# Self-attention stages reordered, head projection in one loop, semaphores cleared in groups

## The chip, the cores and the metric

The program runs on 1 core of a Trainium2 chip. The metric is its time on the device in microseconds (us). It is written in Bass: each engine (TensorE or PE, VectorE or DVE, ScalarE or ACT, GpSimd or POOL, SyncE or SP for DMAs) has an instruction queue of its own, and semaphores alone order one engine against another.

## The reference

Twelve residual layers on x of 32 x 64 tokens x 256 features, each on a layer norm of x. Two of them matter here:

```python
# L1_attn (retention): q, k, v of 16 heads x 16; the (q k) weights are multiplied by a decay matrix,
#   applied to v, normed per batch row and head (mean, variance), scaled, projected with wo
# L2_attn: x + softmax(q k / scale) v Wo + bo, with
def _rmsnorm(x, w):
    rms = jnp.mean(xf * xf, axis=-1, keepdims=True)
    return xf / jnp.sqrt(rms + 1e-06) * w
# q = _rmsnorm(heads of x Wq + bq, wq), k the same; v = x Wv + bv; attention inside each row of 64 tokens
```

## The kernel before

x stays in SBUF as 16 tiles of 128 tokens (2 batch rows of 64) x 256 features. The program is a chain of 34 stages (`stage`, line 31). A stage allocates its tiles and semaphores and opens a `Block` with one instruction list for each engine. The block ends with a barrier of all engines; after it `stage` has GpSimd clear the stage's semaphores (L53) and all engines meet in a second barrier (L54). Weights that outlive a stage are in `held` objects, loaded in the layer norm ahead of their use (`loads=`); that stage can also run their preparation on GpSimd (`prepare=`). Inside a stage the order of each engine is written out by hand, as the order of calls of small helpers (`take(i)`, `flip(i, n)`), i being the tile.

`normed_heads` (L2540) makes queries, keys and values of the second attention. It has two passes over the 16 tiles: first projection in plain fp32 (L2570), bias and squares; then one root and one reciprocal over all tiles (L2591, L2624), and a second loop that scales (DVE, L2628), transposes on PE (L2578, called flip) and stores (ACT, L2596). GpSimd first sets the value tile l2a_v to zero in one instruction (L2558), for which the first values have to wait.

`softmax_attention` (L2632) has per tile: 32 score matmuls on 32 of the 128 rows of the array (`scores`, L2701), maximum and subtraction on DVE (`take`, L2786 and L2790), exponentials on ACT (L2758), their sums and reciprocal on DVE (`add_up`, L2796), scaling on GpSimd (L2675), 8 transposes on all 128 rows (`flip`, L2712), copies of their halves by ACT and DVE (`turned`, L2763 and L2804), 64 matmuls on 64 rows (`attend`, L2726), copies by ACT (`attended`, L2768), 4 matmuls on all 128 rows (`output`, L2736), and the update of x (L2808). The bias of x is added on GpSimd in 4 instructions (L2683) ahead of the first scaling.

`retention_attention` (L2832) has `attend`, `scores`, a matmul for the means (L2905) and one for the variances (L2909), which share one PSUM tile, and `output`. So the matmul of the means of tile i waits until DVE has taken the variances of tile i-1 (`variance`, L3004).

Of the kernel before, what the change touches and what calls it, by code (L numbers as in the profile page):

```python
# [13 lines left out]
P = 128  # L14
BATCH = 32
SEQ = 64
DIM = 256
# [10 lines left out]

@contextmanager
def stage(nc):  # L30
# [22 lines left out]
    nc.clear_and_free_semaphores(sems)  # L53
    nc.all_engine_barrier()  # L54
# [335 lines left out]
class HeadWeights:  # L390

    def __init__(self, sb, sem, d):
        self.d = d
        self.W, self.B, self.WQK = sb("nh_w", [P, KC, 3 * DIM]), sb("nh_bias_rows", [P, 3 * DIM]), sb("nh_rms_weights", [P, 2])
        self.s_w = sem("weights_loaded")

    def load(self, sp):
        d = self.d
        sp.dma_start(self.W[:, :, :], rows_to_sbuf(d["L2_attn_WqkvT"])).then_inc(self.s_w, 16)
# [2140 lines left out]
def normed_heads(nc, XNT, QKT, VA, ident, held):  # L2540

    with stage(nc) as (sb, ps, sem):
        W, B, WQK, s_w = held.W, held.B, held.WQK, held.s_w
        RAW = sb("nh_qk", [P, TILES, 2 * DIM])
        sq = [sb("nh_squares", [P, 2 * DIM]) for _ in range(2)]
        R = sb("nh_rms", [P, TILES, 32])
        psQ = [ps("nh_psq", [P, 512]) for _ in range(2)]
        psV = [ps("nh_psv", [P, 512]) for _ in range(2)]
        psF = [ps("nh_psf", [P, 4, P]) for _ in range(2)]
        s_one, s_p, s_b, s_v, s_sq, s_r = (sem("ones_set"), sem("projected"), sem("qk_ready"),  # L2550
                                                sem("values_ready"), sem("squares_ready"), sem("squares_summed"))
        s_d, s_rt, s_rt2, s_n, s_f, s_out = (sem("dve_step"), sem("mean_squares_ready"), sem("roots_ready"), sem("normed"),
                                             sem("flipped"), sem("stored"))
        with nc.Block() as block:
            @block.gpsimd
            def _(pool):

                nc.gpsimd.memset(VA[:, :, :, :, :], 0.0).then_inc(s_one, 1)  # L2558
                pool.wait_ge(s_one, 1)

            @block.tensor
            def _(pe):

                pe.wait_ge(s_w, 48)
                for t in range(TILES):
                    if t >= 2:
                        pe.wait_ge(s_v, t - 1)
                    for dst, lo, hi in ((psQ[t % 2][:, :], 0, 2 * DIM), (psV[t % 2][:, 0:DIM], 2 * DIM, 3 * DIM)):
                        for c in range(KC):
                            last = nc.tensor.matmul(dst, XNT[:, c, t * P:(t + 1) * P], W[:, c, lo:hi], start=(c == 0),  # L2570
                                                    stop=(c == KC - 1))
                    last.then_inc(s_p, 1)
                for t in range(TILES):
# [3 lines left out]
                    for m in range(4):  # L2577
                        last = nc.tensor.transpose(psF[t % 2][:, m, :], RAW[:, t, m * P:(m + 1) * P], ident[:, :])  # L2578
                    last.then_inc(s_f, 1)

            @block.scalar
            def _(act):
                act.wait_ge(s_w, 48)
# [1147 lines left out]
```

## Time and profile before

| | us |
|---|---|
| time before, median of 3 runs (lowest, highest) | 2920.92 (2920.48, 2927.56) |
| the profiled execution: its time | 2934.49 |
| its span, first to last instruction | 2932.7 |
| PE, DVE, ACT, POOL busy | 2515.0, 1735.1, 1383.3, 637.7 |
| mean granted TensorE clock | 0.922 of 2.4 GHz |

A stage starts when the one before has ended, so the span is a sum of stages, and each stage has its own limit. The granted clock is 1.0 (2.4 GHz) or 0.5 (1.2 GHz); a mean between them is a mixture of both. The stages of the change lie at 1578.7 to 1677.3 (retention), 2194.9 to 2205.5 (layer norm ahead of the heads), 2205.6 to 2276.6 (heads) and 2277.1 to 2389.9 (softmax).

### The profile page before, as it was taken

Reading aid. Unit: us, or ns where it says so; the run is one execution under the profiler, and the core shown is the slowest. Engines: PE = TensorE matmul, PEld = TensorE weight load, DVE = VectorE, ACT = ScalarE, POOL = GpSimd, SP = SyncE. Lnnn points to the kernel's source line nnn. Section 1 sums busy time; section 2 is a strip of 40 time slices with the busy share of each in tenths; the row PEclk is TensorE's granted clock in tenths of the full one; section 3 lists DMA queues with packets and bytes.
Section 4 is the critical chain, followed back from the end, with each engine's and each line's share of the span. In section 5 each row is a group of like instructions: output and inputs, shape, how many; then the busy total and the mean of one; then the engine's idle time right before and its main releaser. Section 6 shows DMA issues by size and latency. Waiting matters only on the chain. (4 is left out here: it accounts for less than half of the span.)

```text
span 2932.7 us, 83514 instructions
## 1 busy us (share of the span) xinstructions
PE 2515.0 (86%) x35763; PEld 2110.2 (72%) x35763; DVE 1735.1 (59%) x3396; ACT 1383.3 (47%) x3431; POOL 637.7 (22%) x826
## 2 busy tenths in 40 slices
PE   6999788999958999999987739977998666999888
PEld 4888455777747999899976539965765554999567
DVE  5777675566655433333335645557885676777663
ACT  3888324455532444444431314426873343777441
POOL 3111002211103200000002122322330534655300
PEclk8999899999989999999998559987998688999999
DMA  2110003212031000000000032332321001111100
GB/s 74 38 35 20 16 7 87 60 32 60 3 90 56 16 17 16 16 16 17 2 24 1 25 126 92 117 105 81 92 78 36 2 2 40 51 51 52 44 1 29
DMA packets 118221, 126.65 MB, mean 43 GB/s; under 512 B 10877, under 2 KB 110153, under 8 KB 117865
## 3 DMA queue, kind: packets, MB, share of 16 engines
q1 hardware_dynamic: 114024, 110.93, 12.3%
q0 software_dynamic: 3840, 10.49, 1.2%
q8 instruction: 282, 4.62, 0.6%
q14 instruction: 75, 0.61, 0.1%
HBM read 105.67 MB, written 15.73 MB: 41 GB/s over the span
## 5 line engine op out<-in xcount | busy, mean ns | idle before, releaser
L1012 ACT ACTIVATE s_ca_probs<-s_ca_scores,s_ca_neg_max 128x256 f32<-128x256 f32 x768 | 353.4, 478 | 36.7 <-DVE s_ca_neg_max L1056 26.1
L1056 DVE TENSOR_REDUCE s_ca_neg_max<-s_ca_scores 128x4 f32<-128x1024 f32 x192 | 234.3, 1222 | 54.6 <-PE s_ca_scores L918 26.8
L935 PE MATMUL s_ca_probs_flipped<-identity,s_ca_probs 128*128 128x128 f32 x1536 | 213.6, 283 | 11.5 <-ACT s_ca_probs L1012 10.5
L2045 DVE COPY s_mx_w_mixed<-s_mx_ps 128x512 f32<-128x512 f32 x256 | 163.6, 684 | 95.4 <-PE s_mx_ps L1892 80.5
L935 PEld LDWEIGHTS s_ca_probs_flipped<-identity,s_ca_probs 128*128 128x128 f32 x1536 | 167.7, 143 | 50.3 <-ACT s_ca_probs L1012 23.2
L2000 ACT COPY s_mx_w_mixed<-s_mx_ps 128x512 f32<-128x512 f32 x256 | 137.2, 589 | 118.6 <-PE s_mx_ps L1879 97.9
L1012 ACT ACTIVATION_READ_ACCUMULATOR s_ca_probs<-s_ca_scores,s_ca_neg_max 128x1 f32 x768 | 160.1, 208 | 0.0
L604 PE MATMUL s_ln_flip<-identity,s_ln_xn 128*128 128x128 f32 x352 | 63.3, 362 | 110.1 <-DVE s_ln_xn L586 109.8
L1019 ACT COPY s_ca_probsT<-s_ca_probs_flipped 128x512 f32<-128x512 f32 x192 | 115.3, 600 | 79.5 <-PE s_ca_probs_flipped L935 79.5
L75 PE MATMUL s_cc_shared<-s_cc_ctxT_low,h_cc_wkv_high 128*128 128x256 f32 x512 | 146.0, 285 | 2.2 <-DVE s_cc_ctxT_low L1407 2.2
L839 POOL TENSOR_TENSOR s_ca_inv_spread<-s_ca_inv_sums,h_ca_own_half 128x128 f32<-128x128 f32 x192 | 72.9, 401 | 343.9 <-DVE s_ca_inv_sums L1078 343.9
L76 PE MATMUL s_cc_shared<-s_cc_ctxT_high,h_cc_wkv_low 128*128 128x256 f32 x512 | 144.4, 282 | 0.0
L77 PE MATMUL s_cc_shared<-s_cc_ctxT_high,h_cc_wkv_high 128*128 128x256 f32 x512 | 144.2, 282 | 0.0
L604 PEld LDWEIGHTS s_ln_flip<-identity,s_ln_xn 128*128 128x128 f32 x352 | 59.3, 193 | 115.2 <-DVE s_ln_xn L586 113.5
L1062 DVE COPY s_ca_probsT<-s_ca_probs_flipped 128x512 f32<-128x512 f32 x192 | 131.0, 682 | 16.6 <-PE s_ca_probs_flipped L935 16.6
L1365 ACT COPY s_cc_kT<-s_cc_shared 128x512 f32<-128x512 f32 x128 | 75.1, 586 | 117.3 <-PE s_cc_shared L77 117.3
L284 POOL TENSOR_SCALAR x_normed_transposed<-x_normed_transposed,h_cc_rstd,h_cc_shift 128x256 f32<-128x256 f32 x56 | 30.7, 559 | 450.8 <-PE s_cc_out L1301 276.0
L1421 DVE RECIPROCAL s_cc_inv_sums<-s_cc_out 128x8 f32<-128x8 f32 x32 | 6.7, 208 | 183.8 <-PE s_cc_out L1301 183.8
L75 PE MATMUL s_cc_shared<-h_cc_wkv_low,s_cc_ctxT_high 128*128 128x512 f32 x256 | 107.4, 419 | 0.8 <-issue 0.8
L958 PE MATMUL s_ca_out<-s_ca_probsT,h_ca_v_spread 128*32 128x64 f32 x6144 | 106.5, 221 | 1.0 <-DVE s_ca_probsT L1062 1.0
L958 PEld LDWEIGHTS s_ca_out<-s_ca_probsT,h_ca_v_spread 128*32 128x32 f32 x6144 | 91.0, 110 | 17.4 <-issue 17.4
L77 PE MATMUL s_cc_shared<-h_cc_wkv_high,s_cc_ctxT_high 128*128 128x512 f32 x256 | 101.1, 395 | 0.0
(500 smaller groups left out, 7383.0 us busy)
## 6 DMA issues: line engine op xcount, KB each, us to landing
h_ca_ctxT<-in_ctxT SPq DMA_DIRECT2D x96, 256.0 KB, 3.4
h_mx_w_by_input<-in_L_ffn_eW1T SPq DMA_DIRECT2D x16, 512.0 KB, 5.4
h_mx_w_by_hidden<-in_L_ffn_eW2T SPq DMA_DIRECT2D x8, 1024.0 KB, 6.3
h_re_win<-in_L_ffn_W_in SPq DMA_DIRECT2D x8, 1024.0 KB
h_ca_ctx<-in_ctx SPq DMA_DIRECT2D x32, 256.0 KB, 2.8
x_normed_transposed<-in_ctx SPq DMA_DIRECT2D x7, 1024.0 KB, 6.4
h_re_wout<-in_L_ffn_W_out SPq DMA_DIRECT2D x8, 512.0 KB
choice_results<-s_rt_zeros SPq DMA_DIRECT2D x4, 1024.0 KB, 10.8
```

Source lines behind the costliest of these rows:

```text
L75: nc.tensor.matmul(dst, lhs[0], rhs[1], start=start, stop=False)
L76: nc.tensor.matmul(dst, lhs[1], rhs[0], start=False, stop=False)
L77: return nc.tensor.matmul(dst, lhs[0], rhs[0], start=False, stop=stop)
L604: last = nc.tensor.transpose(flip[u % 4][:, c, k, :], XN[:, t, c * P:(c + 1) * P], ident[:, :])
L935: last = nc.tensor.transpose(psT[u % len(psT)][:, 2 * a + c, :], PR[b % 2][:, 4 * n + 2 * h + a, c * P:(c + 1) * P], ident[:, :])
L958: last = nc.tensor.matmul(psO[32 * r:32 * r + 32, g * SEQ:(g + 1) * SEQ], V[b % 2][:, c, g * NR + r, 2 * h:2 * h + 2, :].rearrange("p a d ...
L1012: last = nc.scalar.activation(PR[b % 2][:, p, :], psS[:, p // 2, (p % 2) * NKEY:(p % 2 + 1) * NKEY], ACT.Exp, bias=nmax[b % 2][:, p:p + 1] ...
L1019: nc.scalar.copy(PT[b % 2][:, 4 * n:4 * n + 2, :, :].rearrange("p a c q -> p (a c) q"), psT[u % len(psT)][:, :, :]).then_inc(s_ta, 1)
L1056: nc.vector.tensor_reduce(nmax[b % 2][:, 4 * n:4 * n + 4], psS[:, 2 * n:2 * n + 2, :].rearrange("p r (g k) -> p r g k", g=GR), AX_X, ALU.m ...
L1062: nc.vector.tensor_copy(PT[b % 2][:, 4 * n + 2:4 * n + 4, :, :].rearrange("p a c q -> p (a c) q"), psT[u % len(psT)][:, :, :]).then_inc(s_ ...
L2000: last = nc.scalar.copy(part(int(name[1]), r), bank(j, r))
L2045: last = nc.vector.tensor_copy(part(int(name[1]), r), bank(j, r))
```

## The change

Four parts. (1) `stage` collects the semaphores of finished stages and clears them, with the second barrier, only when 64 or more are pending; the barrier inside the block stays. (2) In the retention stage, `variances(i-1)` and `variance(i-1)` come ahead of `scores(i+1)` and `decay(i+1)`. (3) The heads' stage becomes one loop on all engines: the weights are split into high and low fp32r parts by GpSimd in the layer norm ahead (`prepare`), the input likewise per tile (ACT and GpSimd), the projection is three fp32r passes, and root, reciprocal, scaling (now on GpSimd) and flip follow tile by tile, the flip 3 tiles behind. Per step ACT does `square(t)`, `root(t-1)`, `high(t+3)`, `store(t-3)`, DVE `take(t)`, `sum_squares(t)`, `invert(t-1)`; raw tiles stand in 4 buffers, split input tiles in 3. (4) In the softmax stage, PE's and DVE's order is rewritten, and GpSimd adds the bias between tiles.

```diff
 def stage(nc):
-    nc.clear_and_free_semaphores(sems)
-    nc.all_engine_barrier()
+    _pending.extend(sems)
+    if len(_pending) >= PENDING:        # PENDING = 64
+        nc.clear_and_free_semaphores(list(_pending))
+        nc.all_engine_barrier()
+        _pending.clear()
 class HeadWeights:
+    def prepare(self, pool):
+        pool.wait_ge(self.s_wq, 16)
+        for c in range(KC):
+            pool.tensor_copy(self.WH[:, c, :], self.W[:, c, :]).then_inc(self.s_wh, 1)
+            pool.wait_ge(self.s_wh, c + 1)
+            pool.tensor_tensor(self.WL[:, c, :], self.W[:, c, :], self.WH[:, c, :].bitcast(F32), ALU.subtract).then_inc(self.s_wl, 1)
...
 def normed_heads:                       # POOL
+                nc.gpsimd.memset(eps[:, :], 1e-6).then_inc(s_eps, 1)
+                low(0)
+                for q in range(4):
+                    nc.gpsimd.memset(VA[:, 4 * q:4 * q + 4, :, :, :], 0.0).then_inc(s_one, 1)
+                    if q == 0:
+                        low(1)
+                low(2)
+                for t in range(TILES):
+                    normalise(t)
+                    if t + 3 < TILES:
+                        low(t + 3)
+                for t in range(TILES + LAG):        # PE
+                    if t < TILES:
+                        project(t)
+                    if t >= LAG:
+                        flip(t - LAG)
...
 def softmax_attention:                  # PE
-                for i in range(TILES + 2):
+                for i in range(1, TILES + 2):
                     if i >= 2:
+                        attend(i - 2)
                         output(i - 2)
-                    if 1 <= i <= TILES:
+                    if i + 1 < TILES:
+                        scores(i + 1)
+                    if i <= TILES:
                         flip(i - 1, 0)
                         flip(i - 1, 1)
-                        attend(i - 1)
-                    if i + 2 < TILES:
-                        scores(i + 2)
...
 def retention_attention:                # PE; DVE has the same move of variance(i - 1) ahead of decay(i + 1)
                     attend(i)
+                    if i:
+                        variances(i - 1)
                     if i + 1 < TILES:
                         scores(i + 1)
-                    if i:
-                        variances(i - 1)
                     means(i)
```

How the queues stand in a row, at three places.

PE in the softmax loop (L2701 scores, L2736 output, L2712 flip, L2726 attend), one tile and the start of the next, before:

```order
L2736 MATMUL s_sm_pso<-h_sm_wo,s_sm_attendedT 128x256 x2
L2712 MATMUL s_sm_pst<-identity,s_sm_probs 128x128 x8
L2726 MATMUL s_sm_pso<-s_sm_probsT,l2a_v 32x64 x32
L2701 MATMUL s_sm_pss<-l2a_qkT,s_sm_q_spread 128x64 x16
L2736 MATMUL s_sm_pso<-h_sm_wo,s_sm_attendedT 128x256 x2
```

and of the change:

```order
L2789 MATMUL s_sm_pso<-s_sm_probsT,l2a_v 32x64 x32
L2799 MATMUL s_sm_pso<-h_sm_wo,s_sm_attendedT 128x256 x2
L2764 MATMUL s_sm_pss<-l2a_qkT,s_sm_q_spread 128x64 x16
L2775 MATMUL s_sm_pst<-identity,s_sm_probs 128x128 x8
L2789 MATMUL s_sm_pso<-s_sm_probsT,l2a_v 32x64 x32
```

The output, which was followed by the flips, is now followed by the scores; attend and output, which had the scores between them, are neighbours.

DVE in the same loop, one tile, before:

```order
L2786 TENSOR_REDUCE s_sm_max<-s_sm_pss 128x16
L2790 TENSOR_TENSOR s_sm_scores<-s_sm_pss,s_sm_max 128x1024
L2808 TENSOR_TENSOR x_resident<-s_sm_pso,x_resident 128x256
L2804 COPY s_sm_probsT<-s_sm_pst 128x512
L2796 TENSOR_REDUCE s_sm_sums<-s_sm_exponentials 128x16
L2800 RECIPROCAL s_sm_inv_sums<-s_sm_sums 128x16
L2812 BN_STATS x_statistics<-x_resident 128x6
```

and of the change:

```order
L2849 TENSOR_REDUCE s_sm_max<-s_sm_pss 128x16
L2853 TENSOR_TENSOR s_sm_scores<-s_sm_pss,s_sm_max 128x1024
L2871 TENSOR_TENSOR x_resident<-s_sm_pso,x_resident 128x256
L2875 BN_STATS x_statistics<-x_resident 128x6
L2859 TENSOR_REDUCE s_sm_sums<-s_sm_exponentials 128x16
L2863 RECIPROCAL s_sm_inv_sums<-s_sm_sums 128x16
L2867 COPY s_sm_probsT<-s_sm_pst 128x512
```

The copy of the flipped half moved behind the sums, to the end of the tile.

GpSimd from the layer norm ahead into the heads' stage, of the change (before, the stage has one MEMSET of l2a_v 128x8192 and nothing else):

```order
L417 TENSOR_TENSOR h_nh_w_low<-h_nh_w,h_nh_w_high 128x768
L561 UNCONDITIONAL_BRANCH
L59 ISA x5
L2575 UNCONDITIONAL_BRANCH
L2587 MEMSET s_nh_eps 128x1
L2579 TENSOR_TENSOR s_nh_x_low<-x_normed_transposed,s_nh_x_high 128x256
L2590 MEMSET l2a_v 128x2048
L2579 TENSOR_TENSOR s_nh_x_low<-x_normed_transposed,s_nh_x_high 128x256
L2590 MEMSET l2a_v 128x2048 x3
L2579 TENSOR_TENSOR s_nh_x_low<-x_normed_transposed,s_nh_x_high 128x256
L2585 TENSOR_TENSOR s_nh_qk<-s_nh_qk,s_nh_rms 128x512
L2579 TENSOR_TENSOR s_nh_x_low<-x_normed_transposed,s_nh_x_high 128x256
```

The low part of the third input tile (L2579) now stands behind all four clears of l2a_v, and each later one behind a scaling (L2585).

## Rows read from the trace of the kernel before

**Rows 1.** stretch, length, busy PE PEld DVE ACT POOL, PEclk, DMA share, GB/s
```profile
2205.60:2276.60 71.00, 56.05 (x192) 33.99 (x192) 39.77 (x66) 23.78 (x49) 6.90 (x1) 0.88 0.02 9
2277.10:2389.90 112.80, 79.45 (x1728) 67.04 (x1728) 83.28 (x113) 33.91 (x65) 57.91 (x52) 0.77 0.01 2
1578.70:1677.30 98.60, 74.52 (x1664) 54.79 (x1664) 58.76 (x162) 31.28 (x96) 18.90 (x32) 0.60 0.01 2
2280.00:2319.00 39.00, 26.64 (x412) 22.77 (x408) 25.46 (x30) 8.58 (x15) 24.14 (x19) 0.50 0.01 1
2320.00:2329.00 9.00, 7.15 (x213) 6.35 (x214) 8.29 (x13) 2.62 (x7) 4.65 (x4) 1.00 0.02 4
```
**Rows 2.** line 53, and the two barriers behind the heads' stage
```profile
L53 POOLq EVENT_SEMAPHORE_RANGE_CLEAR  x34: 44/91/177, 11.8 to 2931.4; - x34
L2554 PEldq EVENT_SEMAPHORE  x1: 51/51/51, 2276.6 to 2276.6; - x1
L54 PEldq EVENT_SEMAPHORE  x1: 51/51/51, 2277.1 to 2277.1; - x1
```
**Rows 3.** waits of the retention stage: us in total, times, longest
```profile
PE s_rn_psm L2905 <- DVE s_rn_vars L3004: 15.6, 15, 1.2
```
**Rows 4.** timeline and DMA of the layer norm ahead of the heads: start, us
```profile
2197.20 5.26 DVE L586 TENSOR_SCALAR s_ln_xn<-x_resident,s_ln_mean,s_ln_rstd 128x256 f32<-128x256 f32 x16
...
h_nh_w<-in_L_attn_WqkvT SPq DMA_DIRECT2D x1, 768.0 KB, 4.3
```
**Rows 5.** timeline of an earlier layer norm with GpSimd copies beside it
```profile
1989.51 5.94 DVE L586 TENSOR_SCALAR s_ln_xn<-x_resident,s_ln_mean,s_ln_rstd 128x256 f32<-128x256 f32 x16
1991.83 1.31 POOL L173 COPY h_ca_v_spread<-h_ca_ctx 128x256 f32<-128x256 f32 x2 [2.68 <-DMA h_ca_ctx<-in_ctx]
```
**Rows 6.** GpSimd operations by form: x count, busy us, mean ns
```profile
L183 POOL TENSOR_TENSOR h_ca_wkv_low<-h_ca_wkv,h_ca_wkv_high 128x1024 fp32r<-128x1024 f32 x2 | 4.9, 2434 | 0.2
L181 POOL CAST h_ca_wkv_high<-h_ca_wkv 128x1024 fp32r<-128x1024 f32 x2 | 2.8, 1375 | 0.0
L2675 POOL TENSOR_TENSOR s_sm_probs<-s_sm_exponentials,s_sm_inv_sums 128x1024 f32<-128x1024 f32 x16 | 30.5, 1904 | 46.1 <-DVE s_sm_inv_sums L2800 46.1
```
**Rows 7.** tiles of the heads' stage: x count, ns min/median/max
```profile
L2614 DVE TENSOR_TENSOR s_nh_qk<-s_nh_psq,h_nh_bias_rows x16: 681/692/692, 2212.9 to 2252.1; 128x512 f32 x16
L2589 ACT ACTIVATE s_nh_squares<-s_nh_qk x16: 629/631/632, 2213.7 to 2252.9; 128x512 f32 x16
...
L2607 DVE TENSOR_REDUCE s_nh_rms<-s_nh_squares x16: 675/680/687, 2214.8 to 2253.6; 128x512 f32 x16
```
**Rows 8.** timeline, the heads' stage: first GpSimd operation
```profile
2205.57 6.93 POOL L2558 MEMSET l2a_v<- 128x8192 f32 x1 [10.51 <-POOLq L54]
```
**Rows 9.** timeline, fp32r matmuls of the first projection
```profile
34.45 0.39 PE L77 MATMUL s_pj_out<-s_pj_x_part,s_pj_w_part 128*128 128x512 f32 x1
34.68 0.40 PE L75 MATMUL s_pj_out<-s_pj_x_part,s_pj_w_part 128*128 128x512 f32 x1
```
**Rows 10.** timeline, softmax loop, one tile at the low clock
```profile
2304.96 1.17 PE L2726 MATMUL s_sm_pso<-s_sm_probsT,l2a_v 64*32 64x64 f32 x64 [0.83 <-issue]
2307.97 2.08 PE L2736 MATMUL s_sm_pso<-h_sm_wo,s_sm_attendedT 128*128 128x256 f32 x4
2309.84 1.91 PE L2712 MATMUL s_sm_pst<-identity,s_sm_probs 128*128 128x128 f32 x8
2312.58 1.17 PE L2726 MATMUL s_sm_pso<-s_sm_probsT,l2a_v 64*32 64x64 f32 x64 [0.83 <-issue]
```
**Rows 11.** timeline, softmax loop: attend of tiles 0, 4, 5, 13
```profile
2297.33 1.17 PE L2726 MATMUL s_sm_pso<-s_sm_probsT,l2a_v 64*32 64x64 f32 x64 [1.40 <-DVE s_sm_probsT L2804]
...
2325.72 0.85 PE L2726 MATMUL s_sm_pso<-s_sm_probsT,l2a_v 64*32 64x64 f32 x64 [1.64 <-DVE s_sm_probsT L2804]
2331.20 0.85 PE L2726 MATMUL s_sm_pso<-s_sm_probsT,l2a_v 64*32 64x64 f32 x64 [1.65 <-DVE s_sm_probsT L2804]
...
2377.87 0.85 PE L2726 MATMUL s_sm_pso<-s_sm_probsT,l2a_v 64*32 64x64 f32 x64 [1.71 <-DVE s_sm_probsT L2804]
```

More of the change, by code:

```diff
@@ L2569, in _, with flip @@
                         for c in range(KC):
[L2570 to L2571 removed]
+                            last = three_passes(nc, dst, (XH[t % NX][:, c, :], XL[t % NX][:, c, :]), (WH[:, c, lo:hi], WL[:, c, lo:hi]),
+                                                c == 0, c == KC - 1)
                     last.then_inc(s_p, 1)
[L2573 removed]
+                def flip(t):
                     pe.wait_ge(s_n, t + 1)
@@ new lines, in square, with root, store @@
+                def square(t):
+                    act.wait_ge(s_b, t + 1)
+                    if t >= 2:
+                        act.wait_ge(s_r, t - 1)
+                    nc.scalar.activation(sq[t % 2][:, :], RAW[t % 4][:, :], ACT.Square).then_inc(s_sq, 1)
+                def root(t):
+                    act.wait_ge(s_r, t + 1)
+                    nc.scalar.activation(R[:, t, :], R[:, t, :], ACT.Sqrt, bias=eps[:, 0:1], scale=1.0 / 16).then_inc(s_rt, 1)
+                def store(t):
+                    act.wait_ge(s_f, t + 1)
+                    for m in range(2):
+                        last = nc.scalar.activation(QKT[:, 2 * m:2 * m + 2, t * P:(t + 1) * P], psF[t % 2][:, 2 * m:2 * m + 2, :], ACT.Copy,
+                                                    scale=WQK[:, m:m + 1])
+                    last.then_inc(s_out, 1)
@@ L2600, in _ @@
+                for t in range(NX):
+                    high(t)
+                act.wait_ge(s_w, 32)
+                act.wait_ge(s_eps, 1)
+                for t in range(TILES + LAG):
+                    if t < TILES:
+                        square(t)
+                    if t and t <= TILES:
+                        root(t - 1)
+                    if t + NX < TILES:
+                        high(t + NX)
+                    if t >= LAG:
+                        store(t - LAG)
             @block.vector
@@ new lines, in sum_squares, with invert @@
+                def sum_squares(t):
+                    dve.wait_ge(s_sq, t + 1)
+                    nc.vector.tensor_reduce(R[:, t, :], sq[t % 2][:, :].rearrange("p (h d) -> p h d", d=16), AX_X, ALU.add).then_inc(s_r, 1)
+                def invert(t):
+                    dve.wait_ge(s_rt, t + 1)
+                    nc.vector.reciprocal(R[:, t, :], R[:, t, :]).then_inc(s_ri, 1)
+                dve.wait_ge(s_w, 32)
+                for t in range(TILES + 2):
+                    if t < TILES:
+                        take(t)
+                        sum_squares(t)
+                    if 1 <= t <= TILES:
+                        invert(t - 1)
@@ L3535, in perceiver @@
     _names.clear()
+    _pending.clear()
     kept = []
```

138 lines of the change are left out of this document (62 added, 76 removed).

## The prediction

> **What bounds the kernel now.** First the stretches with their clock. The stages follow one another behind barriers, so what one gains or loses goes straight into the span. Of 2932.7 us the change touches four stages: heads 71.0, softmax 112.8, retention 98.6 [rows 1] and the layer norm ahead of the heads, some 10.6. The reader should look at PEclk: heads 0.88, softmax 0.77, retention 0.60. The clock is one of two levels, 1.2 or 2.4 GHz, and in these small loops it sets how long a tile takes. In the softmax stage the first 39 us stand at 0.50 and the tiles behind them mostly at 1.00 [rows 1]. The attends of tiles 0 to 2 are 7.62 us apart (2304.96 to 2312.58) [rows 10], those of tiles 4 and 5 only 5.48; over 13 tiles it is 80.54/13 = 6.20 [rows 11].
>
> Then the waits and the timeline, stage by stage. In retention PE waits 15 times, 15.6 us in all, for DVE's variances ahead of the matmul of the means [rows 3]. In the heads' stage DVE cannot start before GpSimd's clear of 6.93 us is over [rows 8], and a second pass follows the first. Behind each stage stand a clear and a second barrier [rows 2].
>
> **Semaphores.** From the end of the block's barrier (2276.6) to the end of the second one (2277.1) is 0.5 us [rows 2]; 34 such are some 18 us. The change keeps 6 plus the last. A clear is 44 to 177 ns, 91 in the middle [rows 2], and grows with what it clears; a grouped one is 3 to 5 instructions, so I take 1.0 us for each of the 6 and 0.6 more for the last, which holds 5. Saved 17.5 - 6 - 0.6 = 11. If the barrier hid something that the next stage needs anyway (its branch, its first load) it is less: bounds -5 and -15. I take **-11**.
>
> **Retention.** With variances ahead of the scores, their result reaches DVE while PE does scores, so the wait of 15.6/15 = 1.04 per tile ends. What is late next, at 1.2 GHz, is PE itself, with no pause left in a tile; at 2.4 GHz it is DVE. Against that stands the clock: mean 0.60, so it rises now and then, in a stretch of means, output and attend without a pause. If the new loop stays at 1.2 GHz it loses those quick tiles: 14 tiles at (6.2 - 1.1) = 5.1 instead of the mean 5.8 is about -9. If it rises as often as now, the whole 15.6 goes; if it stays up, some 22. I take **-9**, bounds -7 and -22.
>
> **Layer norm ahead of the heads.** GpSimd splits the weights: twice a cast of 768 columns (1.375 x 0.75 = 1.03) and a subtraction (2.434 x 0.75 = 1.83), 5.7 us [rows 6], from about 2199.3 (stage start 2195.0, landing 4.3 [rows 4]) to 2205. By itself that fits, since the stage ends at 2205. But DVE is then in its 16 scalings, 2197.20 to 2202.46 [rows 4], and these suffer: in an earlier layer norm two GpSimd copies, 0.41 each alone, took 1.31 and the same 16 scalings took 5.94 instead of 5.26 [rows 5]. So 0.82 of GpSimd cost DVE 0.68, five sixths. Of 5.7 that would be 4.7, and PE and ACT behind DVE move with it. I take **+4.5**, bounds 0 and +6. The Trainium skill, "SBUF — State Buffer", section "Who interferes with whom", says it more harshly: a tensor_scalar in its two-port mode and a GpSimd operation lock one another out for the whole instruction; by that all 5.7 would be lost, +5.7. The trace agrees in kind, with 0.68 for 0.82.
>
> **Heads in one loop.** PE: a 512-column fp32r matmul follows the last after 0.23 us [rows 9]; six of these and six of half the width are 2.1 us, the flip 0.5, so PE is not the limit at 2.4 GHz. The limit is a ring of waits. The low part of tile t+3 stands on GpSimd behind the scaling of tile t; that waits for the reciprocal of t, which DVE does behind the sum of t+1; that needs projection t+1. One turn, which moves two tiles: add 0.69, square 0.63, sum 0.68 [rows 7], reciprocal 0.25, scaling 1904/2 = 0.95 and low part 2434/4 = 0.61 to 0.75 [rows 6], projection with its drain 2.25, and seven hand-overs of 0.05 to 0.13, together 0.5: 6.6, so 3.3 per tile. At the start the third low part waits for the four clears, 6.93 [rows 8], and two low parts: it is ready at about 9.8, and tiles 2 and 3 are projected at 14 (16 if PE starts at 1.2 GHz). Six turns of 6.6 make 54 to 56, the last tile's way through scaling, flip and store 5.2, the barrier 0.5: 61.5 against 71.0. I take **-9.5**. Bounds: -13 (GpSimd operations shorter), +11 (the loop at 1.2 GHz, a rival below).
>
> **Softmax.** At the start GpSimd's bias additions no longer stand ahead of the first scaling, but the third scores then wait for the second spread and for PE's new order; take(2) moves by less than half a us. The loop is what counts. Today's tile at 1.2 GHz (7.62): output, flips, copy, attend, scores. The new one is a ring through all of it: attend 1.17, ACT's copy 0.52 with hand-overs, output 1.87 (2307.97 to 2309.84), scores 1.91, flips 1.92 [rows 10], DVE's copy and its hand-overs 0.83: 8.22. In the old order scores covered ACT's copy; now nothing does. At 2.4 GHz DVE is the limit: 5.48 today [rows 11], and with the sums directly behind the update and the statistics only 0.75 of work covers the exponential's 1.15, so 5.75. Either way a tile is not shorter.
>
> Which level holds decides the price. Scores use 32 rows of the array and attend 64 x 32, output and flips all 128 x 128 [rows 10]. The rise at about 2319.5 came straight behind an output and its flips with nothing between, and 39 us of low clock were spent with PE busy 26.64 of 39 [rows 1] before it. The new order puts the scores between output and flips, so the longest stretch at full array falls from 3.8 us to 1.9, with pauses on both sides of attend. The stage still starts low, since PE waits for GpSimd and DVE between the first scores. I expect that it now never leaves 1.2 GHz: 13 tiles x (8.22 - 6.20) = 26, and the tail, which now runs at 2.4 GHz, +1.5. I take **+27.5**. Bounds: -14 (2.4 GHz throughout, 5.75 per tile and a shorter start and tail), +31.
>
> **Sum.** -11 - 9 + 4.5 - 9.5 + 27.5 = +2.5 on an execution of 2934.49. That execution is 13.6 above the median, 2920.92, so I count the difference on the median: **2923**. A difference under 0.3% (8.8 us) can't be told from none here.
>
> **Rivals.**
> (A) The softmax loop rises as now. For it: it is a pattern of phases, and a tile's pauses move. Against it: no output-flip pair is left. Then 3 low tiles in the beginning and one slow stretch in five give about 5.75 x 0.75 + 8.22 x 0.25 = 6.4 per tile, +2.5 instead of +27.5: 2898.
> (B) Both attention loops stay at 2.4 GHz: softmax -12, retention -20, the rest as above: 2934.5 - 48 in the profile's frame, 2872. For it: both loops have shorter single pauses at 2.4 GHz. Against it: retention is at 0.60 now.
> (C) Slower. The heads' loop stays at 1.2 GHz: its pauses of about 1.4 us per turn keep it there. Then PE is the limit, 3.9 for a projection and 0.95 for the flip: 16 x 4.85 + 4 = 82, +11 instead of -9.5: 2943. It decides as soon as more than half of the tiles run low. Against it: the present projection, with pauses as well, is at 0.88 for the stage [rows 1].
> (D) The grouped clears save little, because the block's barrier absorbs it: -4 instead of -11: 2930, within 0.3%.
>
> **Chances.** The forecast with the loop held low (D inside it) 0.63, of which about 0.08 falls below 2912 and 0.08 above 2930; A 0.24; B 0.07; C 0.06. Faster: 0.08 + 0.23 + 0.07 = 0.38. Slower: 0.08 + 0.05 = 0.13. The same: 0.49. The range reaches to A and ends short of B and C: 2892 to 2935; the likeliest case alone is 2913 to 2934.
>
> **What would show it.** Softmax: attends 8.2 us apart and PEclk 0.50 for the whole stage (A: 5.75 in most). Retention: the wait of line 2905's matmul gone, tiles 5.1 apart at 0.5. Layer norm: DVE's 16 scalings over 9 us long, the stage 4 to 5 us longer. Heads: one stage of 61 us, with GpSimd's low part 9.8 us in and pairs of projections 6.6 apart. Barriers: 7 instead of 34. I am wrong if PEclk in the softmax stage is well above 0.5, or if a heads' tile needs 4.8.

## The result, and the profile after

The changed kernel took 2916.36 us (median of 20 runs) where before took 2921.70 beside it. The ratio is 0.9966, 95% interval 0.9953 to 0.9979: 9.9 us faster (6.1 to 13.7). One of the 20 runs took 3666.9 us at a mean clock of 0.633 and is left out of the ratio; without it the means are 2913.6 and 2923.5, which lie further apart than the medians. The forecast was "no change" at 2923; the time lies inside its range of 2892 to 2935, but the interval of the ratio leaves out "no change". The profiled execution took 2912.91, its span is 2911.1 us.

The four stages of the change after it: retention, layer norm ahead of the heads, heads, softmax (stretch, length, busy PE PEld DVE ACT POOL, PEclk, DMA share, GB/s). They answer to [rows 1].

```profile
1574.50:1649.80 75.30, 56.74 (x1664) 42.33 (x1664) 55.30 (x162) 30.50 (x96) 18.95 (x32) 0.85 0.01 3
2147.90:2162.00 14.10, 7.81 (x32) 6.23 (x32) 11.06 (x23) 6.50 (x11) 5.84 (x5) 0.58 0.77 261
2161.90:2224.90 63.00, 48.66 (x256) 39.40 (x256) 31.61 (x64) 30.35 (x80) 35.08 (x37) 0.91 0.00 1
2225.00:2366.90 141.90, 109.79 (x1728) 86.27 (x1728) 84.60 (x113) 34.55 (x65) 57.98 (x52) 0.53 0.01 2
```

Against the stages of before (98.6, some 10.6, 71.0 and 112.8) that is -23, +3.5, -8 and +29. Of the other thirty stages, whose inside the change doesn't touch, two thirds differ by less than 1 us; the rest differ by more, from 11.8 us shorter to 2.5 longer. The largest of these differences is in the stage of `routed_experts`, 231.8 us before and 220.0 after; over all 18 profiles it took 219.3 to 221.8 us in nine and 226.9 to 232.9 in the other nine, with kernels built on before and on the changed one in both groups. Why is open. So one pair of profiles (-21.6) can't be used as the effect; the times can.

**Barriers.** The clear and the second barrier after, lines 59 and 60 (ns min/median/max, first and last start), against [rows 2]:

```profile
L59 POOLq EVENT_SEMAPHORE_RANGE_CLEAR  x26: 45/132/262, 428.7 to 2901.2; - x26
...
L60 SPq DRAIN  x6: 7/7/7, 428.7 to 2899.8; - x6
L60 PEldq EVENT_SEMAPHORE  x6: 51/51/51, 429.8 to 2901.6; - x6
```

There are 6 of them instead of 34. The first takes from 428.6 to 429.8, 1.2 us; the last, which clears most, 1.9. All 34 of before take 18.0 us in the trace, the 6 of after 8.7: 9.3 saved. Behind the last stage stands the program's own last clear, now with the leftover semaphores: 0.95 us before, 1.54 after.

**Retention.** Of the wait of 15.6 us for DVE's variances [rows 3] 0.4 is left. PE now waits at another place, 0.8 us a tile for DVE's centred values (us in total, times, longest):

```profile
PE s_rn_pso L2958 <- DVE s_rn_centered L3053: 11.8, 14, 1.5
```

The first 17 us run low, the next 51 at the full clock, in spite of this pause:

```profile
1576.00:1593.00 17.00, 12.23 (x334) 9.48 (x334) 9.31 (x21) 2.94 (x10) 6.21 (x11) 0.52 0.01 3
1594.00:1644.00 50.00, 39.83 (x1272) 29.96 (x1259) 42.91 (x130) 24.64 (x80) 11.87 (x20) 1.00 0.02 4
```

In the timeline the matmuls of the means (L2967; the rows are their weight loads) follow one another after 3.87 us, with the variances' (L2971) between:

```profile
1602.81 0.30 PEld L2967 LDWEIGHTS s_rn_psm<-s_rn_row_sums,h_rn_same_head 128*128 128x128 f32 x2 [0.17 <-issue]
...
1605.74 0.30 PEld L2971 LDWEIGHTS s_rn_psm<-s_rn_square_sums,h_rn_same_head 128*128 128x128 f32 x2 [0.16 <-DVE s_rn_square_sums L3060]
...
1606.68 0.30 PEld L2967 LDWEIGHTS s_rn_psm<-s_rn_row_sums,h_rn_same_head 128*128 128x128 f32 x2 [0.17 <-issue]
```

**Layer norm ahead of the heads.** DVE's 16 scalings (L602) took 5.26 [rows 4] and now 9.81; beside them stand GpSimd's casts (L415) and subtractions (L417) of the weights:

```profile
2150.34 9.81 DVE L602 TENSOR_SCALAR s_ln_xn<-x_resident,s_ln_mean,s_ln_rstd 128x256 f32<-128x256 f32 x16
...
2153.14 1.02 POOL L415 CAST h_nh_w_high<-h_nh_w 128x768 fp32r<-128x768 f32 x1 [4.93 <-DMA h_nh_w<-in_L_attn_WqkvT]
...
2154.24 1.87 POOL L417 TENSOR_TENSOR h_nh_w_low<-h_nh_w,h_nh_w_high 128x768 fp32r<-128x768 f32 x1
...
2156.06 1.03 POOL L415 CAST h_nh_w_high<-h_nh_w 128x768 fp32r<-128x768 f32 x1
...
2157.16 1.87 POOL L417 TENSOR_TENSOR h_nh_w_low<-h_nh_w,h_nh_w_high 128x768 fp32r<-128x768 f32 x1
```

Four of the 16 scalings stand beside these four operations (line 602 from 2153.7 to 2158.9, ns min/median/max):

```profile
L602 DVE TENSOR_SCALAR s_ln_xn<-x_resident,s_ln_mean,s_ln_rstd x4: 1049/1546/2035, 2153.2 to 2157.2; 128x256 f32<-128x256 f32 x4
```

The two beside a cast take 1.05 and 1.06 us, the two beside a subtraction 2.03 and 2.04, and each ends 0.15 behind its neighbour. The other twelve take 0.40 to 0.42. So the whole growth of 4.55 us lies in these four.

**Heads.** The ring that the prediction describes: DVE takes projection t (L2670) in pairs, and the low part (L2579) stands behind the scaling (L2585) on GpSimd. From 2178.57 to 2185.19 two tiles take 6.62 us:

```profile
2178.57 0.69 DVE L2670 TENSOR_TENSOR s_nh_qk<-s_nh_psq,h_nh_bias_rows 128x512 f32<-128x512 f32 x1 [0.57 <-PE s_nh_psv L84]
...
2180.98 1.06 POOL L2585 TENSOR_TENSOR s_nh_qk<-s_nh_qk,s_nh_rms 128x512 f32<-128x512 f32 x1 [1.16 <-DVE s_nh_rms L2681]
...
2182.00 0.74 POOL L2579 TENSOR_TENSOR s_nh_x_low<-x_normed_transposed,s_nh_x_high 128x256 fp32r<-128x256 f32 x1
...
2182.27 0.69 DVE L2670 TENSOR_TENSOR s_nh_qk<-s_nh_psq,h_nh_bias_rows 128x512 f32<-128x512 f32 x1 [1.37 <-PE s_nh_psv L84]
...
2185.19 0.69 DVE L2670 TENSOR_TENSOR s_nh_qk<-s_nh_psq,h_nh_bias_rows 128x512 f32<-128x512 f32 x1 [0.58 <-PE s_nh_psv L84]
```

**Softmax.** One tile at 1.2 GHz on PE, attend to attend 8.41 us (attend, output, scores, flips, attend):

```profile
2292.37 1.17 PE L2789 MATMUL s_sm_pso<-s_sm_probsT,l2a_v 64*32 64x64 f32 x64 [0.83 <-issue]
2294.07 2.07 PE L2799 MATMUL s_sm_pso<-h_sm_wo,s_sm_attendedT 128*128 128x256 f32 x4 [0.53 <-ACT s_sm_attendedT L2831]
2296.07 1.98 PE L2764 MATMUL s_sm_pss<-l2a_qkT,s_sm_q_spread 32*128 32x64 f32 x32
2297.99 1.97 PE L2775 MATMUL s_sm_pst<-identity,s_sm_probs 128*128 128x128 f32 x8
2300.78 1.17 PE L2789 MATMUL s_sm_pso<-s_sm_probsT,l2a_v 64*32 64x64 f32 x64 [0.83 <-issue]
```

### The profile page after: what moved, and what is told of

Read it like the earlier page. It is cut to its first block and busy times, and to the rows that moved or that the text cites. A ratio compares the mean times of both kernels' runs of the same rounds, so it can differ in the third digit from the quotient of the medians.

```text
span 2911.1 us, 83185 instructions
## 1 busy us (share of the span) xinstructions
PE 2512.6 (86%) x35827; PEld 2115.3 (73%) x35827; DVE 1730.6 (59%) x3394; ACT 1391.4 (48%) x3462; POOL 676.1 (23%) x866
## 5 line engine op out<-in xcount | busy, mean ns | idle before, releaser
L951 PE MATMUL s_ca_probs_flipped<-identity,s_ca_probs 128*128 128x128 f32 x1536 | 213.0, 282 | 11.5 <-ACT s_ca_probs L1028 10.6
L83 PE MATMUL s_cc_shared<-h_cc_wkv_high,s_cc_ctxT_low 128*128 128x512 f32 x256 | 101.1, 395 | 0.9 <-issue 0.9
## 6 DMA issues: line engine op xcount, KB each, us to landing
choice_results<-s_rt_zeros SPq DMA_DIRECT2D x4, 1024.0 KB, 10.6
```

What stands on the lines that cost most here:

```text
L83: nc.tensor.matmul(dst, lhs[1], rhs[0], start=False, stop=False)
L951: last = nc.tensor.transpose(psT[u % len(psT)][:, 2 * a + c, :], PR[b % 2][:, 4 * n + 2 * h + a, c * P:(c + 1) * P], ident[:, :])
```

## The experiments

There were sixteen experiments, in four sessions with runs of before beside each; one is the changed kernel again (e5) and one a repetition (e15); ratios are to before of the same session. The prediction was wrong in its sum, so the first question is which term. A gain in us is what the ratio lacks to 1, times the median of before in its session; where two kernels of different sessions are compared, it is by these ratios.

**1. The grouped clears alone (e1).** Before, with `stage` of the change.

```diff
-    nc.clear_and_free_semaphores(sems)
-    nc.all_engine_barrier()
+    _pending.extend(sems)
+    if len(_pending) >= PENDING: ...   # clear, barrier
```

> The kernel before with the grouped clears alone (7 second barriers instead of 34). My theory: the 27 that go cost 0.5 us each and nothing hides them, so 10 to 12 us less than before (about 2911 where before has 2922), every stage of the profile about 0.4 us shorter and none changed in its inside. Rival D of the prediction (the barrier of the block absorbs it): 4 us less or nothing. A third view: the stages start at another phase of the clock, and the time moves by more than 12 us either way.

Measured 0.9947 (0.9929 to 0.9966), 15.5 us faster (10 to 21). The theory of 10 to 12 stands in the interval; the rival with 4 us is out, the third view (more than 12 us) is not. The clears' own rows show 9.3, so up to 6 us may be noise or later stages starting at another moment.

**2. Retention order alone (e2).** Before, with the order of the change in this one stage (DVE's `variance` moves with it).

```diff
                     attend(i)
+                    if i:
+                        variances(i - 1)
                     if i + 1 < TILES:
                         scores(i + 1)
-                    if i:
-                        variances(i - 1)
```

> The kernel before with the retention stage's new order alone. Theory after the result: the clock rises in this stage and stays up, since the pause ahead of the means is gone; stage 75 to 80 us instead of 99, 20 to 24 us less than before. Rival 1 (the term as predicted): the stage stays mostly at 1.2 GHz and is some 90 us long, 9 us less. Rival 2: the stage is sometimes at one level and sometimes at the other, whatever the order; the gain over many executions is then between, about 10 to 15 us, and the spread between executions is wider than before.

Measured 0.9933 (0.9913 to 0.9953): 19.6 us faster (14 to 26). The stage:

```profile
1580.60:1657.60 77.00, 58.66 (x1664) 43.83 (x1664) 55.71 (x162) 30.52 (x96) 18.93 (x32) 0.82 0.01 3
```

All 14 profiles in which this stage has the new order show 74.0 to 77.0 us at 0.82 to 0.88, the three with the old order and no filler 98.5 to 99.1 at 0.60 or 0.61. In e1, with the old order, the stage ahead has the same length and mean clock as here (21.8 us, 0.84), so what ran ahead doesn't explain it. The term of the forecast, -9, is refuted.

**3. The retention stage with its pause filled (e9).** Before, old order and old wait, one more matmul where PE waits (the result is overwritten).

```diff
                         variances(i - 1)
+                    if i >= 2:
...
+                        nc.tensor.matmul(psY[:, 0:DIM], SH[:, :], WO[:, 0, :], start=True, stop=True)
                     means(i)
```

> The kernel before with one more matmul per tile in the retention stage (128x128 weights, 256 columns, its result overwritten by the output behind it), put where PE waits for the variances ahead of the means. The order and the wait stay. Theory: the stage ran low because of PE's pause there; with the pause filled (0.93 us at 1.2 GHz against a wait of 1.04) the clock rises and the stage is 78 to 86 us instead of 99 although it computes more. Rival: the order of variances and scores is what counts (or the wait as such); then the clock stays at 0.6 and the stage is 99 us or longer.

Whole stage, and its part from 1608.7:

```profile
1587.80:1668.50 80.70, 62.03 (x1692) 44.50 (x1692) 57.53 (x162) 31.27 (x96) 18.84 (x32) 0.89 0.01 3
1608.70:1668.50 59.80, 48.00 (x1304) 33.92 (x1292) 47.02 (x137) 26.96 (x83) 11.83 (x20) 1.00 0.01 3
```

The stage computes more, keeps its wait, and is 18 us shorter, with the clock at 1.00 from 1608.7 on. So it is PE's pause ahead of the means that kept the clock down, not the order as such: experiment 2 removes it without added work, this one fills it without a new order. Over all executions the gain was only 8.8 us (0.9970, 0.9951 to 0.9988). In some of them the clock may have risen later, or other stages may have taken longer, as `routed_experts` does; no profile shows which.

**4. The changed kernel with the old retention order (e13).**

```diff
                     attend(i)
-                    if i:
-                        variances(i - 1)
                     if i + 1 < TILES:
                         scores(i + 1)
+                    if i:
+                        variances(i - 1)
```

> The changed kernel with the retention stage's old order. Theory: the stage is back at 98.5 us, so this kernel loses 22 us against the changed one and is about 12 us slower than before (ratio 1.003 to 1.006): the whole error of the forecast was the retention term, since 2923 + 13 (the mis-sized part) comes out of the other terms. Rival: the gain of the retention stage is partly given back by the stages behind it; then the kernel loses only 10 us against the changed one (ratio about 0.999).

Ratio 1.0003 (0.9975 to 1.0032), median 2933.16 beside 2927.25. The interval is wide since 3 of 12 executions took 2898 to 2913 and the rest 2930 to 2940. Undoing the part (DVE's order with it) loses 11 us by the ratios against the result and 13 against experiment 5, with intervals of about 2 to 20 and 2 to 23 that still hold the 19.6 of experiment 2. It loses 12 to 14 where only executions that stay low in the softmax stage are compared (their median is 7.9 us above before here, 4.2 and 6.3 below for the changed kernel in its two sessions). Between the theory (1.003 to 1.006) and the rival (0.999) this lies in the middle and doesn't decide. The split in two groups led to the next question.

**5. The changed kernel once more (e5),** without an edit.

> The changed kernel itself once more, beside the kernels that are compared with it. If the four measured parts add up (clears -11 to -14, retention -21, layer norm +4.5, heads -9, softmax +27), it is 9 to 13 us faster than before. Theory on the softmax stage: at 1.2 GHz throughout, 142 us. Rival: the stage's clock hangs on the moment at which it starts, and in some executions it rises in the middle, as it did behind the old heads' stage (124 us); then executions of about 2893 stand beside those of 2916.

Ratio 0.9960 (0.9936 to 0.9984), 11.7 us faster, within the 9 to 13 to which the parts add up. This time the profile fell on the other outcome of the softmax stage. Three stretches, then the whole stage:

```profile
2260.00:2270.00 10.00, 8.24 (x172) 6.47 (x172) 6.77 (x10) 2.09 (x5) 4.24 (x6) 0.50 0.01 2
2270.00:2280.00 10.00, 8.08 (x152) 6.25 (x152) 8.09 (x11) 3.77 (x8) 4.99 (x4) 0.88 0.01 2
2280.00:2290.00 10.00, 7.17 (x202) 5.49 (x201) 8.85 (x14) 3.77 (x8) 8.41 (x7) 1.00 0.01 3
2243.60:2352.10 108.50, 75.26 (x1728) 59.60 (x1728) 83.35 (x113) 34.39 (x65) 57.94 (x52) 0.85 0.01 2
```

Until 2272 the loop runs low; then the clock rises and stays up until 2344, when the loop has all but ended. The attends (L2789) are now 5.56 us apart, near the 5.75 that the prediction had worked out for 2.4 GHz:

```profile
2292.45 0.85 PE L2789 MATMUL s_sm_pso<-s_sm_probsT,l2a_v 64*32 64x64 f32 x64 [0.97 <-ACT s_sm_probsT L2826]
...
2298.01 0.85 PE L2789 MATMUL s_sm_pso<-s_sm_probsT,l2a_v 64*32 64x64 f32 x64 [0.89 <-ACT s_sm_probsT L2826]
```

The same instructions in the same order took 142 us in one execution and 108.5 in another. By the total times, 2 of 19 executions beside the result, 2 of 11 here and 3 of 12 in experiment 4 were quick ones (a reading of the times; stage lengths are known for profiled executions only).

**6. The changed kernel with the old softmax stage (e3).**

```diff
-                for i in range(1, TILES + 2):
+                for i in range(TILES + 2):
                     if i >= 2:
-                        attend(i - 2)
                         output(i - 2)
...
```

> The changed kernel with the softmax stage as it was before (order of all engines and the bias additions). Theory: the new order costs 27 us (142 us at 1.2 GHz against 113 in the two profiles), so this kernel is 25 to 30 us faster than the changed one, about 2889 where before has 2922, with the clock of that stage about 0.75 again. Rival: the stage ran low in the changed kernel since it starts behind a shorter heads' stage, not for its order; then it stays near 0.5 and gains only the shorter tile at 1.2 GHz (7.62 against 8.15 us, 8 us in all), about 2908.

Ratio 0.9875 (0.9854 to 0.9896), 36.7 us faster than before. The stage:

```profile
2239.60:2349.10 109.50, 74.58 (x1728) 63.10 (x1728) 83.16 (x114) 34.11 (x66) 57.98 (x53) 0.82 0.01 2
```

So the new softmax order costs 142 - 109.5 = 32 us where it stays low, and gains 1 where it rises. Over all executions it costs 25 to 27 (36.7 against the 9.9 of the result and the 11.7 of experiment 5), as expected.

**7. The changed kernel with the old heads' stage (e4)** and no split of the weights.

```diff
-                        layernorm_transposed(nc, X, XNT, ident, ST, loads=(h, w, t), prepare=h.prepare)
+                        layernorm_transposed(nc, X, XNT, ident, ST, loads=(h, w, t))
...
```

> The changed kernel with the heads' stage as before (plain fp32 projection, two passes) and without the split of its weights in the layer norm ahead. Theory: it loses the 9 us of the heads' stage and wins back the 3 to 4.5 us of the layer norm, so 4 to 6 us slower than the changed kernel. Rival: heads and layer norm cancel (within 2 us of the changed kernel). The softmax stage should stay at 0.5 as in the changed kernel; if it rises, its clock hangs on what runs ahead of it.

Ratio 0.9935 (0.9916 to 0.9955), by the ratios 7 to 9 us faster than the changed kernel of the other sessions, not slower; the intervals overlap. The profile shows why: heads 72.2 and layer norm 9.2, as expected, but the softmax stage, whose code is untouched, rose at 2322.5 and took 124 us. Whole stage, its low part and its quick part:

```profile
2244.10:2368.30 124.20, 91.55 (x1728) 72.10 (x1728) 83.62 (x113) 34.74 (x66) 57.90 (x52) 0.68 0.01 2
2247.40:2322.50 75.10, 57.87 (x899) 45.82 (x896) 47.64 (x60) 18.39 (x34) 36.57 (x31) 0.50 0.01 2
2322.50:2360.00 37.50, 26.70 (x703) 20.81 (x705) 33.83 (x47) 13.26 (x26) 18.11 (x17) 0.99 0.01 2
```

Experiment 7 therefore says nothing on heads by its time. That the level hangs on the moment at which the stage starts is a guess from it: one profile doesn't show that, since the changed kernel by itself has both outcomes.

**8. PE's order: scores between attend and output (e6).** In the changed kernel:

```diff
                         attend(i - 2)
-                        output(i - 2)
                     if i + 1 < TILES:
                         scores(i + 1)
+                    if i >= 2:
+                        output(i - 2)
```

> The changed kernel with one move in PE's order of the softmax stage: scores between attend and output, so that output and flips are neighbours again and the scores hide ACT's copy. Theory: at 1.2 GHz a tile is 0.5 us shorter (7.7 instead of 8.2), and output with its flips gives PE a stretch without a pause, behind which the clock rises as in the old order: stage 105 to 115 us instead of 142, 27 to 37 us faster than the changed kernel. Rival: the neighbourhood has nothing to do with the clock; the stage stays at 0.5 and is 134 us long, 8 us faster than the changed kernel.

Ratio 1.0037 (1.0023 to 1.0051), stage 156.1 us at a mean of 0.62: both expectations missed. One tile, from attend to attend:

```profile
2291.50 0.85 PE L2789 MATMUL s_sm_pso<-s_sm_probsT,l2a_v 64*32 64x64 f32 x64 [1.48 <-issue]
...
2292.80 1.19 POOL L2728 TENSOR_TENSOR s_sm_q_spread<-l2a_qkT,s_sm_head_parity 128x256 f32<-128x256 f32 x2
...
2294.03 1.99 PE L2764 MATMUL s_sm_pss<-l2a_qkT,s_sm_q_spread 32*128 32x64 f32 x32 [1.69 <-POOL s_sm_q_spread L2728]
...
2295.95 2.08 PE L2799 MATMUL s_sm_pso<-h_sm_wo,s_sm_attendedT 128*128 128x256 f32 x4
...
2301.07 0.85 PE L2789 MATMUL s_sm_pso<-s_sm_probsT,l2a_v 64*32 64x64 f32 x64 [1.34 <-issue]
```

From attend (2291.50) to the next (2301.07) are 9.57 us. The scores need the spread queries, which GpSimd makes behind its scaling; PE stands for 1.69 us where the output had covered that. The mean of 0.62 is a mixture of both levels in nearly every tile:

```profile
2289.70:2293.10 3.40, 1.17 (x67) 0.80 (x65) 3.33 (x5) 0.74 (x3) 2.16 (x2) 1.00 0.02 5
2293.10:2299.90 6.80, 5.70 (x44) 4.71 (x44) 2.42 (x4) 1.64 (x2) 0.88 (x2) 0.50 0.00 0
2299.90:2303.30 3.40, 0.85 (x64) 0.71 (x64) 3.33 (x5) 0.43 (x2) 2.79 (x3) 1.00 0.03 5
```

The flips end at 2299.73, and the clock rises at 2299.9. So it goes in the whole stage: it rises eleven times, each time within 1 us of the end of an output with its flips, and falls again, in the tiles shown in the pause of 1.7 us behind attend. In the changed kernel PE does the same three groups without a pause, but with the scores between output and flips (the row under "Softmax" above), and the clock stayed at 0.50 for thirteen tiles. So the prediction's reason for the rise (output and flips as neighbours) has support here; it is not enough to keep the level, and experiment 5 shows that the clock can rise without it.

**9. Pauses of PE at the start of the softmax stage filled (e10).** In the changed kernel, 30 transposes of the identity, 6, 10 and 14 ahead of the first three scores:

```diff
+                fill(6)
                 scores(0)
+                fill(10)
                 scores(1)
+                fill(14)
```

> The changed kernel with 30 idle transposes of the identity (128x128) in PE's three pauses at the start of the softmax stage (6, 10 and 14); the loop is untouched. Theory: the new loop keeps the level at which it runs: at 2.4 GHz its pauses are short enough to stay there, at 1.2 GHz it rises seldom (11 of 12 profiles' tiles at 0.5 in one execution, all at 1.0 from the fourth tile in another). With the clock raised before the first tile the stage is 96 to 102 us in nearly every execution instead of 142: 30 to 40 us faster than the changed kernel, about 0.985 of before. Rival (the loop falls back by itself, as the forecast had it): 130 us or more, within 10 us of the changed kernel.

Ratio 0.9859 (0.9825 to 0.9892). Four of six executions took 2869 to 2880, two 2902 and 2910; the profile fell on one of the latter:

```profile
2226.50:2361.80 135.30, 109.95 (x1758) 86.62 (x1758) 84.22 (x113) 34.38 (x65) 57.91 (x52) 0.58 0.01 2
```

So 4 of 6 executions are quick, against 7 of 42 of the changed kernel and of experiment 4. That is few executions; it points to the start, and it doesn't secure them.

**10. Heads without the ring (e7).** Changed kernel with the old softmax stage; on GpSimd `low(t + 3)` ahead of `normalise(t)`, clears between.

```diff
...
                 for t in range(TILES):
-                    normalise(t)
                     if t + 3 < TILES:
                         low(t + 3)
+                    if t < 3:
+                        clear(t + 1)
+                    normalise(t)
```

> The kernel e3_old_softmax (changed, with the old softmax stage) with GpSimd's order in the heads' stage changed: the low part of tile t+3 ahead of the scaling of tile t, and the last three clears of the values between them instead of ahead of the third low part. Theory: the ring low part - scaling - reciprocal - sum - projection sets 3.3 us a tile; without it DVE and PE set about 2.6 and the third low part comes 5 us earlier, so the stage is 50 to 53 us instead of 62.5, 10 us faster than e3_old_softmax (ratio to before about 0.984). Rival: PE is the limit at 1.2 GHz as soon as it works without pauses, or GpSimd itself; the stage gets no shorter than 60.

Ratio 0.9835 (0.9822 to 0.9847); the stage 51.8 us instead of 62.5, as expected:

```profile
2176.30:2228.10 51.80, 44.17 (x256) 37.62 (x256) 31.39 (x65) 30.60 (x81) 35.15 (x38) 0.93 0.00 1
```

How much of this came from the ring and how much from the clears isn't told apart.

**11. Heads projected in plain fp32 in the new loop (e8, e15)**, no split of the weights, old softmax stage. Run in two sessions.

```diff
-                            last = three_passes(nc, dst, (XH..., XL...), (WH..., WL...), ...)
+                            last = nc.tensor.matmul(dst, XNT[:, c, t * P:(t + 1) * P], W[:, c, lo:hi], ...)
```

> The kernel e3_old_softmax with the heads projected in plain fp32, in the new loop (no high and low parts, no split of the weights in the layer norm, clears of the values between the scalings). Theory: projection 2.75 us a tile as before and the flip 0.5 make PE the limit at 3.3 us a tile, the same as the ring of the three-pass version: stage 58 to 61 us; the layer norm is back at 9.2 us instead of 14.1 since GpSimd no longer works beside DVE; together 5 to 8 us faster than e3_old_softmax. Rival: the layer norm was longer for another cause (loads, a later start of its DVE work), then it stays at 14 and the kernel is within 2 us of e3_old_softmax.

> The kernel e8_plain once more, without any filler, beside e14 and e16 on one chip: ratio 0.9805 again. If the start filler gave nothing (0.9819 for e12 against 0.9805 in another session), e16 will not be faster than this one.

Ratios 0.9805 (0.9793 to 0.9818) and 0.9825 (0.9803 to 0.9847). In the second session, layer norm, heads and softmax:

```profile
2148.20:2157.10 8.90, 5.28 (x32) 4.85 (x32) 6.50 (x23) 6.09 (x11) 0.10 (x1) 0.81 0.81 273
2157.10:2212.20 55.10, 50.01 (x192) 31.27 (x192) 31.61 (x64) 25.30 (x64) 23.88 (x21) 0.97 0.07 23
2212.30:2320.70 108.40, 73.45 (x1728) 62.33 (x1728) 83.19 (x113) 34.11 (x65) 57.85 (x52) 0.83 0.01 2
```

The layer norm is back at 8.9 us with nothing else changed in it: GpSimd's split had cost 14.1 - 8.9 = 5.2 (the other profiles with grouped clears and no split have 8.9 to 9.3). The heads take 55.1 instead of 62.5 in e3. The two stages make 12.5 us; by the ratios the kernel is 15 and 20 us faster than e3, more than the 5 to 8 expected. The three-pass projection brought nothing that the ring and the split didn't take: even without the ring (e7) heads and layer norm take 51.8 + 14.1 = 65.9 us, in plain fp32 55.1 + 8.9 = 64.0.

**12. The fillers on top of that.** With the new softmax order: the start alone (e11), then also 2 transposes per tile (e14).

```diff
                         attend(i - 2)
+                        fill(2)
                         output(i - 2)
```

> The kernel e8_plain (heads in plain fp32 in one loop, old softmax order) with the new softmax order and the same 30 idle transposes. Theory: softmax stage 96 to 102 us against 109 to 113 in e8_plain: 8 to 14 us faster than that, ratio to before about 0.976. Rival: the new order falls to 1.2 GHz in this kernel too, since it starts at another moment: 30 us slower than e8_plain, ratio 0.99.

> The kernel e11_plain_new_filler with two more idle transposes per tile, where PE waits for ACT's copy between attend and output. Theory: pauses in the loop are what lets the level fall or keeps it from rising; with this one filled no execution stays low, and the slow ones (2910 in e11, one of six) are gone; time as the quick ones of e11, ratio 0.977 to 0.981. Rival: only the start decides; then slow executions appear as often as in e11, and all are 1 to 2 us longer by the added transposes.

Start alone: 0.9812 (0.9785 to 0.9839), one of six at 2910, the others 2859 to 2874. With the loop filled: 0.9790 (0.9774 to 0.9806), all five at 2860 to 2871. None low of five against one of six doesn't show that the loop filler did anything, and in the profiles both stages are equally long. The softmax stage of the first and of the second:

```profile
2214.10:2314.80 100.70, 74.02 (x1758) 59.46 (x1758) 83.26 (x113) 34.38 (x65) 57.98 (x52) 0.95 0.01 2
```
```profile
2224.20:2325.00 100.80, 79.86 (x1790) 62.56 (x1790) 83.22 (x113) 34.38 (x65) 57.97 (x52) 0.95 0.01 3
```

With the old softmax order, the start alone (e12), then also one matmul per tile where PE waits for the copies (e16):

```diff
                         flip(i - 1, 1)
+                        nc.tensor.matmul(psO[1][:, DIM:2 * DIM], ident[:, :], WO[:, 0, :], start=True, stop=True)
                         attend(i - 1)
```

> The kernel e8_plain with the 30 idle transposes alone, the old softmax order kept. Theory: the 39 us at 1.2 GHz at the start of the stage go, where a tile takes 7.6 instead of 5.5 us: 8 to 10 us less, stage about 101 to 104, ratio to before about 0.977. Rival: the old order falls back to 1.2 GHz soon after the start, since its pauses are longer in the first tiles: no gain against e8_plain (0.9805).

> The kernel e12_plain_old_filler (old softmax order, 30 idle transposes at the start) with one idle matmul of 128x256 per tile where PE waits 1.65 us for the copies of the flipped halves. Theory: the single slow stretches of 3.4 us in the loop (every fifth or so) and the late rise at the start go; stage 97 to 101 us instead of 108 to 113, about 10 us faster than e15_plain_again, ratio 0.977. Rival: the filled pause delays the attends at 1.2 GHz (0.93 us against a wait of 0.83 there) and the clock does not change: same as e15 or slower.

The softmax stage of the first and of the second:

```profile
2220.40:2328.80 108.40, 80.42 (x1758) 68.36 (x1758) 83.13 (x113) 34.10 (x65) 57.94 (x52) 0.83 0.01 2
```
```profile
2217.90:2322.50 104.60, 81.72 (x1790) 68.16 (x1790) 83.02 (x113) 34.41 (x65) 57.91 (x52) 0.89 0.01 3
```

0.9819 (0.9797 to 0.9841) and 0.9802 (0.9788 to 0.9816). The start filler gave nothing: 108.4 us as in the kernel without it. The loop filler took 3.8 us off the stage, not the 10 expected.

The kernel with plain heads, new softmax order and both fillers has the lowest ratio of all: 2865.31 us, 2.1% below before (1.9 to 2.3), where the changed kernel is 0.3% below. The intervals of e8, e11, e12, e15 and e16 overlap with its own.

## Why the prediction was wrong

**Retention, the step that failed.** It was "if the new loop stays at 1.2 GHz": -9 taken, with -22 as the bound if the clock stays up. Behind the first 17 us it stayed up in every profile, the stage is 22 to 25 us shorter, and the part alone brought 19.6 (14 to 26). The prediction had the working for both levels and chose the wrong one, arguing that the loop "loses those quick tiles". It had read the mean clock of 0.60 as a property of the stage. It came from PE's pause of 1.04 us ahead of the means, which the change removed and experiment 3 filled. At the full clock DVE is late next, as the prediction said, and PE's pause of 0.8 us a tile for it didn't bring the clock down.

**Barriers**, -11: 9.3 in the clears' own rows, less 0.6 for the program's own last one, and 15.5 (10 to 21) in the time of the part. Within its bounds, the true size open between these.

**Layer norm**, +4.5: the scalings grew by 4.55, the stage by 5.2 against the same stage without the split. Right. The Trainium skill, "SBUF — State Buffer", section "Who interferes with whom", has the one that issues first hold the shared ports for its whole instruction, while the other is blocked. The trace agrees: the scalings beside the four GpSimd operations end when these end (2.03 us beside a subtraction of 1.87, 1.05 beside a cast of 1.02). The prediction made of it that all 5.7 us would be lost; 4.55 of 5.8 were, since in each of the four stretches DVE still got one scaling done.

**Heads**, -9.5: with its barrier the stage went from 71.6 us to between 62.3 and 63.3. Ring and pairs of 6.6 us are in the trace as worked out, the third low part is ready 11 us into the stage (forecast 9.8), and taking the ring apart and moving the clears gave 10.7 us. Right.

**Softmax**, +27.5: 141.9 us with the clock at 0.53 in the profile, +29 against before and +32 against the old order in the same place. The tile of 8.22 was 8.4 in the row shown. "Never leaves 1.2 GHz" was wrong as a rule: in about 1 of 6 executions the loop rises and then keeps the level, with 5.56 per tile where rival A had 6.4. Retention is up as well, so such an execution is rival B by its mechanism. Forecast and rival are here outcomes of one program, not alternatives. That the term fits the 25 to 27 us over all executions is in part luck: against the old order in the same place the low outcome costs more than forecast (32), and the quick one, which the forecast left out, makes up for it.

**The sum.** With -20 for -9 the prediction's own sum becomes +2.5 - 11 = -8.5, against -9.9 (-6.1 to -13.7) measured. By the experiments: 36.7 saved without the softmax part; with it -36.7 + 32.4 = -4.3 in an execution that stays low and -37.7 in a quick one; one in six quick gives -9.9. The executions above 2900 alone are 4.2 us below before by their median (2917.5), 7.7 by their mean. The part experiments put most of the error into the retention term, 10.6 of some 12 us; how much exactly stays open, since experiment 4 gives only 11 to 14 for the whole term, with a wide interval. Its profile is 24 us longer in this stage; its softmax stage took 135 instead of 142, since the clock rose there 22 us before the end, and its other stages together 9 us more.

## What to carry to other kernels

In these small loops the TensorE clock hung on PE's pauses, so a wait that is removed must be priced at the level that the loop will have without it, and both levels deserve a chance. Where a stage can go either way, take several profiles or read the spread of the times before trusting one stage length. Before moving work to GpSimd, look at what DVE does in the same stretch, and follow GpSimd's own order: the gains here came from taking a subtraction and the clears out of the way, not from adding passes.

## What the runs showed of the hardware

One loop, one program, one chip: 142 us with the clock low and 108.5 with it high from the third tile on. The order counts beside the pauses: scores, output and flips in a row raised the clock eleven times in 16 tiles (e6), output, scores and flips in a row left it at 0.50 for thirteen tiles (the changed kernel's profile). With 30 idle transposes of 128x128 at the start, whose result nobody reads, 4 of 6 executions of the changed kernel were quick. With plain heads as well the stage took 100.7 us at 0.95, and the same with 2 more transposes per tile (100.8), 41 us less than in the profile of the changed kernel, though it computes more; the new order with plain heads and no filler wasn't run.
